# In the last expert stage, one fixed expert's block is added by TensorE with 0/1 matrices instead of through memory and a gather

## The reference

```python
H, I, E_ROUTED, TOP_K = (256, 704, 7, 2)
def _expert(h, g, u, d):
    return jnp.einsum('...i,hi->...h', jax.nn.silu(h @ g.T) * (h @ u.T), d)
shared_out = _expert(x, sg, su, sd)
logits = x @ wr.T + rb
probs = jax.nn.softmax(logits, axis=-1)
scores, idx = jax.lax.top_k(probs, TOP_K)
scores = scores / scores.sum(axis=-1, keepdims=True)
w = jnp.sum(scores[..., None] * jax.nn.one_hot(idx, E_ROUTED, dtype=x.dtype), axis=-2)
out = shared_out
for e in range(E_ROUTED):
    out = out + w[..., e:e + 1] * _expert(x, rg[e], ru[e], rd[e])
```

## Time and profile before

| | |
|---|---|
| median of 3 runs | 832.15 us (830.44, 832.15, 836.06) |
| profiled execution, its own time | 834.35 us |
| span of its instructions | 832.5 us, 12549 instructions |
| PE busy | 755.2 us, 91% of the span |
| DVE, ACT, POOL busy | 42%, 31%, 16% |
| last stage, shared expert's first product to the end | about 664 to 832.5 us |

### The profile page before, as it was taken

One profiled execution on the slowest core, in us unless ns is written; L12 is line 12 of the kernel. 1 busy time (PEld: TensorE's weight loads), 2 busy tenths in 40 slices (PEclk: granted clock), 3 DMA queues, 4 the chain that ended last, 5 costly groups with the idle time before them and its releaser, 6 DMA issues.

```text
span 832.5 us, 12549 instructions
## 1 busy us (share of the span) xinstructions
PE 755.2 (91%) x4399; PEld 591.4 (71%) x4399; DVE 349.5 (42%) x989; ACT 258.1 (31%) x596; POOL 133.1 (16%) x100
## 2 busy tenths in 40 slices
PE   9999899999875698989988979999988999999995
PEld 6687588897533355765754769989975558999984
DVE  3215650001799966568678521111126732111113
ACT  1233244343533313562682212212211112222211
POOL 2000020002069920122050310000040040000004
PEclk9999999999999999999999989999998999999998
DMA  9940016894556420000003509989950423999942
GB/s 325 373 190 1 1 48 203 288 319 142 201 165 156 100 113 0 1 1 1 0 2 127 236 30 308 317 287 320 314 185 2 168 101 118 326 323 318 322 178 86
DMA packets 39267, 139.41 MB, mean 167 GB/s; under 512 B 5696, under 2 KB 20224, under 8 KB 27840
## 3 DMA queue, kind: packets, MB, share of 16 engines
q1 hardware_dynamic: 36992, 133.06, 46.1%
q0 software_dynamic: 2240, 5.90, 2.3%
HBM read 127.58 MB, written 11.35 MB: 167 GB/s over the span
## 4 chain that ended last, share of the span: by engine, by line
PE 59%; DVE 14%; issue 9%; DMA 7%; ACT 3%; POOL 3%; another core or an unknown queue 2%; SPq 1%; DVEq 0%; POOLq 0%; ACTq 0%
PE PS L484 55%; DMA arena<-x_slots 4%; DVE arena L1872 3%; DMA arena<-bc_scratch 2%; POOL arena L1413 1%; PE PS L542 1%; DVE stats L1481 1%; SPq L338 1%; DMA gatew<-gate_w 1%; PE PS L507 1%; DVE stats L1474 1%; POOL arena L1426 1%; DVE arena L1998 1%; ACT XT L1054 1%
## 5 line engine op out<-in xcount | busy, mean ns | idle before, releaser
L484 PE MATMUL PS<-arena 128*128 128x128 f32 (+3 forms) x2442 | 370.4, 310 | 12.9 <-ACT arena L1109 3.4
L484 PEld LDWEIGHTS PS<-arena 128*128 128x128 f32 (+1 forms) x2442 | 326.2, 191 | 44.4 <-issue 10.1
L1682 DVE TENSOR_TENSOR arena<-arena,PS 128x384 f32<-128x384 f32 (+1 forms) x62 | 30.2, 488 | 205.2 <-ACT arena L1096 200.1
L484 PE MATMUL PS<-warm 128*128 128x512 bf16 (+1 forms) x388 | 95.6, 375 | 4.3 <-DVE rs L1465 3.0
L1096 ACT ACTIVATE arena<-PS 128x384 f32<-128x384 f32 x62 | 30.4, 491 | 165.8 <-PE PS L484 161.8
L1400 POOL DMA_INDIRECT arena<-y_slots,posu x25 | 23.6, 944 | 350.0 <-DMA y_slots<-arena 343.3
L484 PEld LDWEIGHTS PS<-warm 128*128 128x128 bf16 x388 | 38.0, 102 | 47.3 <-issue 6.8
L1413 POOL TENSOR_TENSOR arena<-arena 128x1152 f32<-128x1152 f32 x16 | 56.3, 3521 | 33.5 <-DVE arena L1872 33.5
L484 PE MATMUL PS<-arena,ident 128*128 128x512 f32 (+1 forms) x128 | 38.0, 440 | 21.5 <-POOL arena L1413 21.5
L1389 POOL DMA_INDIRECT x_slots<-XH,posu x25 | 24.2, 967 | 182.2 <-DVE posu L1634 175.5
L1694 DVE SCALAR_TENSOR_TENSOR H<-arena,wgt,H 128x256 f32<-128x256 f32 (+1 forms) x25 | 12.0, 480 | 90.2 <-DMA arena<-y_slots,posu 87.5
(11 more groups left out here) (282 smaller groups left out, 862.1 us busy)
## 6 DMA issues: line engine op xcount, KB each, us to landing
arena<-w_moe SPq DMA_DIRECT2D x31, 1152.0 KB, 5.6
arena<-w_moe SPq DMA_DIRECT2D x31, 1024.0 KB, 5.2
arena<-w_moe SPq DMA_DIRECT2D x20, 1026.0 KB, 5.8
arena<-bc_scratch SPq DMA_DIRECT2D x32, 288.0 KB, 3.8
arena<-x_slots SPq DMA_DIRECT2D x41, 128.0 KB, 2.9
y_slots<-arena SPq DMA_DIRECT2D x40, 128.0 KB, 2.0
wx<-w_sh SPq DMA_DIRECT2D x1, 2176.0 KB, 17.6
wsh<-w_moe SPq DMA_DIRECT2D x1, 2052.0 KB, 14.5
```

The costliest lines, as they stand in the source:

```text
L484: return nc.tensor.matmul(out_, l, r, start=start, stop=stop, skip_group_check=True)
L1682: ins = v.tensor_tensor(hid_b[x][:, 0:full], sg_s[x][:, 0:full], PS[:, 2 * x + 1, 0:full], ALU.mult)
```

## The change

ffn3's last block (14) becomes a fixed block of expert 6 (`LASTS["ffn3"]` = 1). The tables in `tri` that turn experts into blocks follow from `LASTS`; there are 15 blocks as before. What moves:

- DVE makes `gate_shares` (now with the weights `comb`), `placed_rows` and `row_weights` between the products of the first shared half, where before `gate_shares` and `row_weights` stood after it.
- PE transposes the matrix, makes two idle products and waits for ACT's copies, ahead of the first routed block.
- Block 14 is not sent to `y_slots`, so the gather waits for block 13 alone.
- After block 14 PE adds it for tiles 0 to 2 (`joined`, three products into PSUM banks 2 and 3); DVE adds those banks to `H` in two instructions after shared product 1 of the second half.
- For tiles 3 and 4 the place product goes into the same PSUM group as the turning back of `YT`, which so becomes two float32 products with the identity and one with `placeT`, instead of two transposes.
- The stores of tiles 0 to 2 may start before the last shared product.

```diff
-LASTS = {"ffn0": 1, "ffn2": 2, "ffn3": 0}
+LASTS = {"ffn0": 1, "ffn2": 2, "ffn3": 1}
...
+        def ACC3(j):
+            return PS[0:TILE_N[j], 2 + j // 2, (j % 2) * D:(j % 2 + 1) * D]
...
                     pe.wait_ge(sem("y_sb"), b + (at + 1 + 2))
+                    if name == "ffn3":
+                        for j in SH_TILES[0]:
+                            mm(ACC3(j), placeT[b - nb][:, tsl(j)], y_s[p]).then_inc(sem("joined"), 1)
+                        return
...
-                        for d in range(KD):
-                            last = nc.tensor.transpose(TM(j)[:, 128 * d:128 * (d + 1)], YT[:, d, tsl(j)], ident[:, :])
+                        if placed:
+                            for d in range(KD):
+                                mm(TM(j)[:, 128 * d:128 * (d + 1)], YT[:, d, tsl(j)], ident[:, :], d == 0, False)
+                            last = mm(TM(j), placeT[-1][:, tsl(j)], y_s[placed - 1], False, True)
+                        else:
+                            for d in range(KD):
+                                last = nc.tensor.transpose(TM(j)[:, 128 * d:128 * (d + 1)], YT[:, d, tsl(j)], ident[:, :])
...
             shared("ffn3", [128] * (CH2 - 1) + [64], (0,), ranked=True)
+            place_transposes("ffn3", NBLK["ffn3"] - 1, 2)
+            idle_products(2)
+            pe.wait_ge(sem("placeT"), LASTS["ffn0"] + LASTS["ffn2"] + 1)
             routed("ffn3")
...
             shared("ffn3", CH2, (0,))
+            place_copies("ffn3", NBLK["ffn3"] - 1, 2)
             routed("ffn3")
...
-            shared("ffn3", CH2, (0,), first=2)
+            gate_shares("ffn3", True, True)
+            for c in range(2, CH2):
+                shared_product("ffn3", CH2, c)
+                if c == 2:
+                    placed_rows("ffn3", 0)
+                if c == 3:
+                    row_weights("ffn3", True)
             side_tiles(8 * NT, 3, range(0, 3))
-            gate_shares("ffn3", True, False)
-            row_weights("ffn3", True)
             routed("ffn3")
-            shared("ffn3", CH2, (1,))
-            for j in range(CH2 - 2, NT):
-                collect_tile("ffn3", j, 2, (3, 2))
-            dve.sem_inc(sem("out_tile"), 3)
+            for c in range(CH2, CH2 + 2):
+                shared_product("ffn3", CH2, c)
+            dve.wait_ge(sem("joined"), NT + 3)
+            mark(v.tensor_tensor(H[:, 0:2, :], H[:, 0:2, :], PS[:, 2, :].rearrange("p (j d) -> p j d", d=D), ALU.add))
+            link(v.tensor_tensor(tile(H, 2), tile(H, 2), ACC3(2), ALU.add))
+            for c in range(CH2 + 2, 2 * CH2):
+                collect_tile("ffn3", c - CH2 - 2, 2, (3, 2))
+                if c == 2 * CH2 - 1:
+                    dve.sem_inc(sem("out_tile"), 3)
+                shared_product("ffn3", CH2, c)
+            collect_tile("ffn3", NT - 1, 2, (3, 2))
```

More of the change, by code:

```diff
@@ L296, in tower @@
         block = ctx.enter_context(nc.Block())
-        COMBS = {"ffn0": 1, "ffn1": 2, "ffn2": 3}
-        PLACED0 = {"ffn0": 0, "ffn2": LASTS["ffn0"]}
-        UNSENT = [NBLK[n] - 1 - i for n in NBLK for i in range(LASTS[n])]
+        COMBS = {"ffn0": 1, "ffn1": 2, "ffn2": 3, "ffn3": 4}
+        PLACED0 = {"ffn0": 0, "ffn2": LASTS["ffn0"], "ffn3": LASTS["ffn0"] + LASTS["ffn2"]}
+        UNSENT = sorted({NBLK[n] - 1 - i for n in NBLK for i in range(LASTS[n])})
         STAGE = {"ffn0": 0, "ffn2": 1, "ffn3": 2}
```

6 lines of the change are left out of this document (2 added, 4 removed).

## The result

| | before | changed |
|---|---|---|
| median of 20 runs each | 833.61 us (827.90 to 840.76) | 839.35 us (834.05 to 844.59) |
| ratio changed / before | | 1.0067, 95% interval 1.0048 to 1.0086 |
| profiled execution, its own time | 834.35 us | 839.94 us |
| span | 832.5 us | 837.8 us |

One execution of each is left out of the extremes, at 1273.51 and 1279.60 us. The change costs 0.67%, some 5.6 us (4.0 to 7.2 by the interval). The forecast was +1.3, at 833.5 us with a range up to 838.0. The size was wrong, and the time is outside the range.

What follows compares the result with a forecast made beforehand. PE, busy for 91% of the span, was taken to bound the kernel. Costs of 3.8 us (a, c, f) against a loss beside the gather shrinking from 5.5 to 3.0 gave +1.3 on 832.15: 833.5 us, range 829.2 to 838.0.

Steps and rivals of the forecast that it cites:

- (a): Ahead of block 0: place transposes, ACT's two copies and a handover delay block 0's transposes on PE's path, +1.6 us.
- (b): First shared half: DVE's matrix rows, `gate_shares` and `row_weights` fit into its 3.3 us waits for ACT, 0 us.
- the scatter rival: Matrix rows beside ffn3's scatter bring the wait seen in ffn2: 4.7 more, +6.0 in all, 838.2 us; chance 0.08.
- (c): Last block: three products of width 256, 0.43 us each, stand ahead of up 0, +1.3 us.
- (d): Last gather: starts after block 13's y copy instead of 14's, at 807.7 instead of 811.23, 3.5 us earlier.
- the loss beside the gather: Second shared half: late silus cost 5.5 us before; with the change it was to shrink to between 3.0 and 3.8.
- the second rival: Lower clock level falls on the second shared half: up to 3.4 us more, +4.7 in all, 836.9 us; chance 0.14.
- The two surcharges: Second shared half: 0.8 us more if silu 2 is held too, and up to 3.4 us for the lower clock level.
- (e): Second shared half: DVE's two additions of `joined` between products 1 and 2, 2.1 us against a 1.95 step, about hidden.
- (f): Tail, turning back of tiles 3 and 4: 2.0 us instead of 1.15, +0.9; at the lower clock level +2.7.
- the change does nothing: Rival: the gather's end doesn't release silu 5, the same 5.5 us is lost, costs paid in full: +3.8, 836.0; chance 0.10.
- no wait: Rival: no wait beside the gather in the changed kernel's second shared half, -1.7 us, 830.4 us; chance 0.28.

Runs made afterwards that it cites:

- on-time sessions: Timing sessions in which the kernel before took about 819 to 823 us and no profile had a silu wait put down to "remote".
- late sessions: Timing sessions in which the kernel before took about 833 us and its profile had silu waits put down to "remote".
- c_after: The changed kernel, unaltered, run again in one of the late sessions: 838.24 us, ratio 1.0067 to the kernel before.
- e2_front: Changed kernel, place transposes behind block 0's own, wait for ACT's copies ahead of its second up, idle products left out; late session: 839.02 us, ratio 1.0077.
- e2b_front: The changed kernel with place transposes moved behind block 0's own transposes, timed in another late session: 840.32 us, ratio 1.0046.
- c_before: The kernel before, unaltered, run again in one of the late sessions: median 833.23 us.
- e7_early: The kernel before with block 14 unsent and the gather waiting for block 13, no added pieces; late session: 833.87 us, ratio 1.0014.
- e9_order: The kernel before with DVE's hidden product put ahead of the gathered additions in the second shared half; late session: 835.68 us, ratio 1.0008.
- c2_before: The kernel before, unaltered, run again in one of the on-time sessions: 822.2 us, ratio 0.9978.
- c2_after: The changed kernel, unaltered, run again in one of the on-time sessions: 825.53 us, ratio 1.0015.
- e5_spaced: The changed kernel with GpSimd waiting for the fifth of ten last-gather loads to land before issuing the other five; one run, on-time session: 821.15 us.
- e5b_spaced: The changed kernel with the same wait behind the fifth load of the last gather, timed in another on-time session: 822.22 us, ratio 1.0000.
- e7b_early: The kernel before with block 14 unsent and the gather started sooner, no added pieces; on-time session: 818.34 us, ratio 0.9926.
- sessions 2 and 5: The two late sessions among the five follow-up timing sessions; the kernel before took 833.23 us and 834.51 us in them.
- e3_idle: The changed kernel with 36 idle products on `warm` ahead of down 2 of the second shared half; one run, on-time session: 828.63 us.

## Why the prediction was right or wrong

**(a) Ahead of block 0, +1.6.** Right: 3.18 us from the `YT` copy to block 0's transposes instead of 1.58. The end of block 14's y copy moved by 1.53 in all, but that this is the same number is luck: the scatter starts 2.86 us earlier in the profile after, which the change has no part in, 0.92 is lost beside it, 1.60 here, and the blocks take 1.86 us more. From block 0's x copy to that y copy the profiles of this case take anything from 117.3 to 122.7 us.

**(b) DVE's pieces hidden, 0.** Half right. The pieces ended inside DVE's waits, and in on-time sessions they cost nothing: the silu in question comes 13.2 us after the scatter's first DMA in every kernel. In late sessions it comes at 14.07 to 14.15 in all four profiles that have the matrix rows there (after, c_after, e2_front, e2b_front), and at 13.2 in all four that have not (before, c_before, e7_early, e9_order). So the scatter rival, with a chance of 0.08 and a price of 4.7 on top of the forecast, came true in its direction with a fifth of its price: 0.92 us, which nothing hides. The profile puts this wait down to PE and not to "remote". Why the matrix rows make the difference is not shown.

**(c) Three products, +1.3.** Right. The first silu of the second half comes 2.95 behind the y copy's end instead of 1.66.

**(d) The gather's start.** Forecast 807.7, measured 808.18; 14.3 after it the release, measured 14.15. This part of the mechanism was right. "What was held before is held again to +14.3" is what happened, and it had a sentence on silu 2 too: 0.8 more. Silu 2 was held.

**What failed** is the sum behind that release: the step "silu 3 is 3.0 late. Then `YT` comes at 828.0", by which the loss beside the gather shrinks from 5.5 to 3.0 us. The copy came at 831.76. Of these 3.8 us, 0.3 is the later release (822.33 for 822.0), 0.8 is silu 2, and the rest, 2.6, is the lower clock level: until 828.05 PE's rows ran at a granted clock of 0.53, and one up took 2.77 us for 1.46. That is the second rival, which had a chance of 0.14 and a price of 3.4. Its condition was named, that PE stands still for about 4 us as before, and the forecast reckoned with a wait of 3.0 by assuming that silu 2 gets through. ACT's wait was 6.76 us and PE stood for 4.39. The two surcharges, 0.8 and the clock, were priced apart, but in the rows they come together: three of the four late profiles with the change hold silu 2 along with 3 and fall to the lower level right behind the release (copy at +21.0, +20.1 and +20.2), and in the fourth, c_after, silu 2 got through and the clock stayed (+16.6). Four profiles are no proof of the order of cause.

The 5.5 us themselves were too many. They set the late kernel before against silus 1.95 us apart, with silu 5 at 819.99; the prediction's own due time for it, +9.7 after the gather's start, is 820.9, and c2_before, with nothing late, has its copy 2.6 us ahead of the late kernel's and not 5.5.

**(e) DVE's additions hidden.** Right: in c2_after, where nothing else is late, they stand there and the silus are 1.95 us apart.

**(f) The tail, +0.9.** It is 6.00 us from the `YT` copy to the end for 4.89, +1.1; 2.27 us from the first turning product to DVE for the 2.0 of the sum.

So the sum by what was measured, place by place, is 1.6 (a) + 0.9 (the scatter) + 1.3 (c) + 1.3 (the copy after block 14's y copy, +21.0 for +18.4, less the joined products) + 1.1 (f) = 6.2, inside the 4.0 to 7.2 us of the times. With the second half as e2_front and e2b_front show it (copy at +20.1 and +20.2) the same sum is 5.3 to 5.4. The forecast had 0 for the second term, and -2.5 for the fourth (+17.2 for +18.4, less 1.3). The spans differ by 5.3, as the stages that the change leaves alone took 1.0 us less in the profile after.

**The rival "the change does nothing"** (0.10, 836.0) is the one that e7_early bears out for late sessions: with the gather 4.6 us sooner and nothing added, the time is the same within 0.4%. I gave it the cause "the gather's end isn't what releases silu 5". That is not what the distances say: eight profiles of five kernels have a release 14.12 to 14.28 us after the first load, the start moved by 4.6 us among them. By its rows the gain is nil for another reason: silus 2 to 4 are held where 4 and 5 were, and PE has more rows left after the release, some at the lower level.

**The rival "no wait"** (0.28, 830.4) was built on a false comparison. "5.5 us are lost beside the gather" took the second half at PE's pace as what the kernel before would do with no lateness. c2_before shows that it isn't: without lateness its copy is at +15.8, as DVE has the last product behind the fourth tile's rows. And the price set a changed kernel without lateness against a kernel before with it. Like against like, in an on-time session, the change is +0.8 by the profiles and 1.0015 by the times. Its premise, that lateness is a property of the kernel, was the error; it goes with the session.

**What a measurement can tell** was put at 1%, 8.3 us. The intervals came out at 0.2 to 0.35% to either side, so that 0.67% is clear of no change.

**The Trainium skill's rule** ("SBUF — State Buffer", section "Who interferes with whom": a DMA never contends with a compute engine) agrees with c2_after, e5_spaced, e5b_spaced and e7b_early of the on-time sessions, where ten indirect DMAs run beside PE with silus 1.95 us apart. The profiles of sessions 2 and 5 have ACT waiting up to 8.13 us for PE's results, where 4.60 is the wait of an on-time session, tied in time to the same kind of DMAs. The rule does not tell these apart.

**What stays open.** Whether the gather causes the lateness in late sessions. Its removal was run three times, each time where nothing was late. That the release keeps its distance to the gather's start is shown; a cause is not, nor whether the first load or the last one sets it, as no late profile has a gather of another length. Nor is it shown why a session is late or not, or how many of the executions behind the median of 839.35 met the lower level in the second half.

No complete version is shown to beat the kernel before: e9_order and e2_front were timed in late sessions only, and e7_early leaves block 14's rows out of the output.

## What to carry to other kernels

A stretch that is released at a fixed distance from some event is not shortened by bringing the event forward under the same work: count what falls behind the release in the new order, and run it at the lower clock level if the wait grows. Before pricing "without the wait", follow every engine's own order in the stretch, since a second bound may stand just behind the first (here DVE's additions ahead of its last product). And compare a rival's condition with the kernel before under that same condition.

## What the runs showed of the hardware

- The same kernel took 818.47 to 828.84 us in one session and 830.08 to 842.05 in another, on what the runs number chip 3 both times. In the slow one ACT waited 6.39 and 7.05 us for PE's results beside ffn2's scatter, where the wait is 2.15 in on-time profiles, and 5.35 and 8.11 us beside its gather, where it is 4.60.
- In late sessions the release comes at nearly the same distance from the first of ten indirect DMAs wherever they stand: 14.12 to 14.28 us in ffn3's gather (eight profiles), 14.28 to 14.40 in ffn2's gather, 14.07 to 14.15 in ffn3's scatter beside the matrix rows (four profiles), 13.44 to 13.49 and once 14.16 in ffn2's scatter. The last DMA is issued 11.3 to 11.5 us after the first. Only results of PE are late: in the profile after, a product of DVE ends at 823.21 and PE goes on at 823.27.
- A run of short products on `warm` that is meant to fill a wait costs its full 3.9 us where the wait is not there (e3_idle).
